# Strassen's algorithm for q, k and v, and attention in 64-wide tiles, in a transformer block in split fp32

## The chip, the cores and the metric

The kernel runs on one core of a Trainium2 chip. Its time is that of one execution on the device, in microseconds (us). TensorE multiplies matrices into PSUM, VectorE and ScalarE read PSUM and SBUF, GpSimd reads SBUF alone, and SyncE issues most of the DMAs.

## The reference

x has 32 sequences of 64 tokens and 1024 features. All in float32:

```
c  = x @ W1.T + b1 + 2 * (x @ A1[id]) @ B1[id]        # LoRA of rank 16, one adapter per sequence
q  = rope(c @ wq)  # 32 heads of 128;  k = rope(c @ wk), v = c @ wv: 8 heads, 4 q heads share one
o  = softmax(causal(q @ k.T / sqrt(128))) @ v         # within each sequence of 64
x1 = x + o @ wo
y  = x1 @ W2.T + 2 * gated LoRA (top 2 of 8 experts, rank 16, bias by language id)
out = x1 + y @ Wf.T + bf + 0.5 * gated residual (top 2 of 16 experts, rank 64)
```

## The kernel before, in words

Every large product is made of three matmuls: a float32 value is split into a high part, rounded to the fast format fp32r, and a low part, the remainder, and `three` (lines 527 to 531) adds hi x hi, hi x lo and lo x hi in PSUM. So a weight tile is loaded raw by SyncE, copied to its high part by ScalarE (`wd`, line 978, and `w_hi`, line 958) and subtracted to its low part by GpSimd (line 1193) or VectorE (`w_lo`, line 1294). There are two slots each for raw, hi and lo. A product bank is 128 outputs x 512 tokens; the four banks `PJ` are used in turn, and a bank is free when VectorE has taken it (the semaphore `taken`).

First, weights are folded once (W2 into Wf) and W1 and others are transposed through TensorE into DRAM scratch (`t_scratch`). Then come two halves of 1024 tokens each (an outer loop over `hf`), each in these stages:

1. The x blocks are loaded (`x_raw`, eight of 128 tokens), turned by TensorE, and split by ScalarE and VectorE; GpSimd adds them up again into x1, in SBUF.
2. The first projection, W1: eight weight tiles, each for two token halves, 24 matmuls and one fp32 LoRA matmul a bank (`w1_block`, line 662). VectorE splits these tiles.
3. Eight groups, one per kv head (loop at line 683): twelve banks of k, v and four q heads (24 matmuls each), with attention spread between them and into the group's output projection, 32 banks of 6 matmuls over the group's four heads, added to x1 by VectorE (line 1434). Attention works on blocks of 128 tokens, two sequences at once, the mask taking away what crosses: per unit of one head and 512 tokens, `score`, `turn_p` and `pv` are four fp32 operations of 128x128 each. VectorE rotates (`rotate`, line 1364), masks and takes maxima (`mask_and_max`), and normalises; ScalarE does the exponentials, copies transposed probabilities, and makes o's high part; VectorE makes its low part.
4. The second projection, its routing, and the output stage, which this change leaves nearly as they were.

Each engine works through its own list in order; only semaphores join them. `hold` puts an instruction of its own behind a wait.

## Time and profile before

| | us |
|---|---|
| median of 3 runs (2927.39 to 2931.74) | 2928.24 |
| span of the profiled execution | 2929.6 |
| TensorE busy in it | 2887.8 |
| VectorE busy | 1516.9 |
| ScalarE busy | 710.9 |
| GpSimd busy | 478.3 |

A matmul's recorded duration overlaps with the next one's, so starts are compared to find what one costs. An instruction's name gives the output and the inputs by the program's names, with the form; "PEld" is the load of a stationary operand. The granted clock is the share of full speed that TensorE was given.

### The profile page before, as it was taken

The page shows a single profiled execution, that of the slowest core. Times are in us where ns is not written, and L with a number is a line of the kernel's source. Part 1 is how long each engine was busy: PE and PEld are TensorE (multiplying, and loading weights), DVE is VectorE, ACT ScalarE, POOL GpSimd, SP SyncE. Part 2 cuts the span into 40 slices and gives each one's busy share as a digit, 9 for nine tenths or more (in the row PEclk, how much of TensorE's full clock was granted, in tenths as well). Part 3 has the DMA queues.
Part 4 walks back from the last instruction along what each step waited for, and adds up shares of the span by engine and source line. Part 5 has one row for each costly group of instructions (what it writes and reads, how often), then busy time and mean ns, then how long its engine had stood idle before and what let it go on. Part 6 is the DMA issues. An engine that isn't in the chain of part 4 may idle for free.

```text
span 2929.6 us, 39491 instructions
## 1 busy us (share of the span) xinstructions
PE 2887.8 (99%) x14200; PEld 2407.0 (82%) x14200; DVE 1516.9 (52%) x2443; ACT 710.9 (24%) x1681; POOL 478.3 (16%) x198
## 2 busy tenths in 40 slices
PE   8989999999999999999998999999999999999999
PEld 7867888888888888887876788888888888888887
DVE  2131656465665646565523265646556474656452
ACT  2121223132221313231102131313223131323110
POOL 0020111211111111110302012111111211111030
PEclk9999999999999999999999999999999999999999
DMA  6841111111111111111442111111111111110232
GB/s 214 233 121 37 43 44 36 43 43 42 37 43 43 36 43 43 37 35 55 111 144 60 43 37 49 37 43 36 43 43 36 44 39 45 37 43 29 72 99 68
DMA packets 230725, 174.67 MB, mean 60 GB/s; under 512 B 65146, under 2 KB 198394, under 8 KB 230658
## 3 DMA queue, kind: packets, MB, share of 16 engines
q1 hardware_dynamic: 202850, 151.80, 18.1%
q10 hardware_dynamic: 27808, 22.02, 2.3%
q8 instruction: 36, 0.59, 0.1%
q14 instruction: 31, 0.25, 0.0%
HBM read 151.58 MB, written 22.22 MB: 59 GB/s over the span
## 4 chain that ended last, share of the span: by engine, by line
PE 89%; DVE 5%; issue 2%; ACT 2%; SPq 1%; DMA 0%; ACTq 0%; DVEq 0%
PE prod L529 26%; PE prod L531 25%; PE prod L530 25%; PE turned L726 4%; PE turned L705 2%; PE turned L715 2%; ACT probs L1051 2%; DVE rope_sin L1372 2%; PE turned L523 1%; PE prod L625 1%; PE prod L888 1%; DVE row_max L1385 1%; DVE probs L1382 1%; PE turned L695 0%; PE prod L865 0%
## 5 line engine op out<-in xcount | busy, mean ns | idle before, releaser
L529 PE MATMUL prod<-c_hi,w_hi 128*128 128x512 f32 (+1 forms) x1856 | 737.7, 397 | 3.2 <-DVE c_lo L1445 3.2
L531 PE MATMUL prod<-c_hi,w_lo 128*128 128x512 f32 (+1 forms) x1856 | 724.3, 390 | 0.0
L530 PE MATMUL prod<-c_lo,w_hi 128*128 128x512 f32 (+1 forms) x1856 | 722.7, 389 | 0.0
L1193 POOL TENSOR_TENSOR w_lo<-raw,w_hi 128x1024 fp32r<-128x1024 f32 x160 | 382.1, 2388 | 1844.1 <-ACT w_hi L983 1844.1
L1434 DVE TENSOR_TENSOR x<-prod,x 128x512 f32<-128x512 f32 x512 | 349.4, 690 | 284.0 <-PE prod L531 281.4
L531 PEld LDWEIGHTS prod<-c_hi,w_lo 128*128 128x128 f32 (+1 forms) x1856 | 347.3, 187 | 75.9
L529 PEld LDWEIGHTS prod<-c_hi,w_hi 128*128 128x128 f32 (+1 forms) x1856 | 347.8, 187 | 74.1 <-DVE c_lo L1445 4.0
L530 PEld LDWEIGHTS prod<-c_lo,w_hi 128*128 128x128 f32 (+1 forms) x1856 | 348.1, 188 | 70.5 <-issue 1.0
L529 PE MATMUL prod<-o_hi,w_hi 128*128 128x512 f32 x1024 | 405.0, 395 | 0.0
L531 PE MATMUL prod<-o_hi,w_lo 128*128 128x512 f32 x1024 | 399.4, 390 | 0.0
L530 PE MATMUL prod<-o_lo,w_hi 128*128 128x512 f32 x1024 | 398.8, 389 | 0.0
L983 ACT CAST w_hi<-raw 128x1024 fp32r<-128x1024 f32 x160 | 167.5, 1047 | 509.1 <-PE prod L531 509.1
L529 PE MATMUL prod<-x_hi,w_hi 128*128 128x512 f32 x656 | 284.2, 433 | 5.4 <-DVE x_lo L1305 1.8
L1051 ACT ACTIVATE probs<-probs,neg_max 128x128 f32<-128x128 f32 x512 | 199.6, 391 | 356.9 <-DVE neg_max L1387 356.9
L531 PE MATMUL prod<-x_hi,w_lo 128*128 128x512 f32 x656 | 257.8, 393 | 0.0
L530 PE MATMUL prod<-x_lo,w_hi 128*128 128x512 f32 x656 | 257.2, 392 | 0.0
L1369 DVE TENSOR_TENSOR rope_cos<-prod,consts_sb 128x512 f32<-128x512 f32 x160 | 110.1, 688 | 246.7 <-PE prod L531 242.7
L531 PEld LDWEIGHTS prod<-o_hi,w_lo 128*128 128x128 f32 x1024 | 192.2, 188 | 41.1
L530 PEld LDWEIGHTS prod<-o_lo,w_hi 128*128 128x128 f32 x1024 | 192.6, 188 | 38.2
L529 PEld LDWEIGHTS prod<-o_hi,w_hi 128*128 128x128 f32 x1024 | 192.5, 188 | 37.9
L1372 DVE TENSOR_TENSOR rope_sin<-prod,consts_sb 64x512 f32<-64x512 f32 x320 | 220.2, 688 | 4.3
L529 PEld LDWEIGHTS prod<-x_hi,w_hi 128*128 128x128 f32 x656 | 124.2, 189 | 43.7 <-issue 18.8
(123 smaller groups left out, 2689.4 us busy)
## 6 DMA issues: line engine op xcount, KB each, us to landing
raw<-in_wq SPq DMA_DIRECT2D x64, 512.0 KB, 4.0
raw<-in_wo SPq DMA_DIRECT2D x64, 512.0 KB, 3.8
raw<-t_scratch SPq DMA_DIRECT2D x34, 512.0 KB, 3.5
t_scratch<-x ACTq DMA_DIRECT2D x17, 512.0 KB, 5.0
x_raw<-in_x SPq DMA_DIRECT2D x16, 512.0 KB, 8.8
raw<-in_wk SPq DMA_DIRECT2D x16, 512.0 KB, 3.6
raw<-in_wv SPq DMA_DIRECT2D x16, 512.0 KB, 3.6
raw<-m_scratch SPq DMA_DIRECT2D x16, 512.0 KB, 3.5
```

Source lines behind the costliest of these rows:

```text
L529: pe.matmul(dst, wh, xh, start=start, stop=False)
L530: pe.matmul(dst, wh, xl, start=False, stop=False)
L531: return pe.matmul(dst, wl, xh, start=False, stop=stop)
L705: mm = pe.matmul(SB_[u % 2][:, b * P:(b + 1) * P], Q[:, (u % 2) * NT + b * P:(u % 2) * NT + (b + 1) * P], K[:, t * NT + b * P:t * NT + (b ...
L715: mm = pe.transpose(TBK[:, b * P:(b + 1) * P], SM[:, c:c + P], ident)
L726: mm = pe.matmul(OB[:, b * P:(b + 1) * P], V[:, (t * BPT + b) * HD:(t * BPT + b + 1) * HD], PT[:, c:c + P], start=True, stop=True)
L983: act.copy(WH[j % 2][:], RAW[j % 2][:]).then_inc(wd_hi, 1)
L1051: ins = act.activation(SM[:, c:c + P], SM[:, c:c + P], ACT.Exp, bias=NMX[:, r:r + 1], scale=SM_SCALE, accum_out=SUM[:, r:r + 1])
L1193: pool.tensor_tensor(WL[j % 2][:], RAW[j % 2][:], WH[j % 2][:].bitcast(F32), ALU.subtract).then_inc(split_d, 1)
L1369: dve.tensor_tensor(view(RC[:, rs], SPT), src, cos, ALU.mult)
L1372: ins = dve.tensor_tensor(view(RS[a:a + hd2, rs], SPT), src[b:b + hd2], sin, ALU.mult)
L1434: dve.tensor_tensor(X1[:, xs], PJ[q % 4][:], X1[:, xs], ALU.add).then_inc(taken, 1)
```

## The change

- **q, k and v by Strassen's algorithm** (in Winograd's form, with shared sums). c is no longer one matrix but seven blocks of 512 features x 512 tokens: b11, b21, b22 and four sums t1 to t4, each split into hi and lo. They are made while W1 runs: W1's tiles are walked twice, first for the first 512 tokens, then for the second (`W1_ORDER`), so there are 16 tile loads a half; VectorE forms the sums. The weights come in pairs of 256 columns (k with v, or two q heads; `load_pair`), 24 pairs a half. GpSimd forms four sums and seven low parts for each pair, ScalarE seven high parts. TensorE makes seven products of 4 x 3 matmuls for a pair (`product`), where there were four banks of 24 matmuls. VectorE combines the seven products into four banks' worth with seven adds, and rotates out of PSUM.
- **Attention per sequence.** Scores are 64x64, two sequences in the two halves of the partitions and two heads side by side; `pv` contracts over the 64 keys of one sequence, for two heads at once. V is transposed a second time, shifted by 64 rows, so that every sequence's rows stand in either half. A group's attention is spread over its last pair and the next group's first two pairs (the last group's over the first output projection banks).
- **o goes through DRAM.** ScalarE copies and stores it in quarters (`o_out`). After the eight groups the output projection runs alone: four blocks of 1024 rows of wo, each of 16 banks x 24 matmuls; o is loaded back and split by ScalarE and GpSimd.
- **x1's start goes through DRAM.** GpSimd adds x's parts up, SyncE stores them (`store_xt`) and loads them before the output projection (`load_x1`).
- **W1's low parts** are made by GpSimd (`tile_lo`), in turn with those sums (`x_back`).
- The halves and groups are written out in full in place of loops, and the next half's first x blocks are turned inside the output stage.

The core of the diff (of the removed lines, the q, k, v loop alone):

```diff
-                    for j in range(12):
-                        main(Q_G + j, (j // TT) % 2, j % TT, CH, CL).then_inc(prod, 1)
...
+W1_ORDER = [(j, 0) for j in range(KC)] + [(j + 4 * s, 1) for j in range(KC // 2) for s in range(2)]
...
+BLOCKS = ["b11", "b21", "t2", "t3", "t1", "t4", "b22"]
+PR_1, PR_2, PR_6, PR_7, PR_5, PR_4, PR_3 = range(7)
...
+LOS = {0: 1, 1: 2, 2: 3, 4: 4, 3: 5, 5: 6, 6: 7}
...
+        places = ["b11", "t2", "b21", "t3", "t1", "t4", "b22"]
+        CBH = {b: sb(f"{b}_hi", [P, 4 * NT], F32R, offset=16 * i * KB) for i, b in enumerate(places)}
+        CBL = {b: sb(f"{b}_lo", [P, 4 * NT], F32R, offset=(16 * i + 8) * KB) for i, b in enumerate(places)}
...
+            def store_xt(hf, b):
+                sp.wait_ge(x_sum, hf * TB + b + 1)
+                sp.dma_start(xt_d.rearrange("k p n -> p k n")[:, :, b * P:(b + 1) * P], view(XS[b % 2][:], KC)
+                             ).then_inc(xt_out[b % 2], 16)
...
+            def load_pair(n, hf, g, qd):
+                if g == 0 and qd == 0:
+                    sp.wait_ge(w_lo, pool_no(hf, T_WO - 1) + 1)
+                else:
+                    sp.wait_ge(s_lo, 7 * (n - 1) + 6)
...
+            def load_o(hf, kb):
+                sp.wait_ge(o_stored, 16 * 4 * (hf * NKV + 2 * kb + 2))
+                if kb == 0:
+                    sp.wait_ge(qprod, q_done(pair_no(hf, NKV - 1, QD_23), 3))
+                elif kb == 1:
+                    sp.wait_ge(o_stored, 16 * 4 * (hf + 1) * NKV)
+                    sp.wait_ge(qprod, q_done(pair_no(hf, NKV - 1, QD_23), 6))
+                else:
+                    sp.wait_ge(prod, qbase(hf) + wo_q(kb - 2, KC - 1, TT - 1) + 1)
+                for c in range(KC):
+                    sp.dma_start(chunk_of(o_lows(kb % 2, OWP), c), o_d[kb * KC + c]).then_inc(o_in[c], 16)
...
+                for n in range(2, T_WO):
+                    if n - 2 < TB:
+                        store_xt(hf, n - 2)
+                    load_w1(hf, n)
...
+                def product(n, i, first):
+                    name, bank = BLOCKS[i], (7 * n + i) % 4
+                    gg, qd = divmod(n, QUADS)
+                    pg, pq = divmod(n - 1, QUADS)
+                    pe.wait_ge(s_lo, 7 * n + LOS[i])
...
+                    hold(pe)
+                    for k in range(4):
+                        if first:
+                            pe.wait_ge(cb_lo, hf * C_N + C_AT[name, k])
+                        ws, xs = slice(k * P, (k + 1) * P), slice(k * NT, (k + 1) * NT)
+                        mm = three(PJ[bank][:], SH[i][:, ws], SL[i][:, ws], CBH[name][:, xs], CBL[name][:, xs],
+                                   k == 0, k == 3)
+                    mm.then_inc(qprod, 1)
...
+                    for b in range(BPT):
+                        for r in range(2):
+                            for s in range(2):
+                                c = b * P + s * SEQ
+                                mm = pe.matmul(SCB[s * SEQ:(s + 1) * SEQ, b * P + r * SEQ:b * P + (r + 1) * SEQ],
+                                               Q[r][t][:, c:c + SEQ], K[:, t * NT + c:t * NT + c + SEQ],
+                                               start=True, stop=True)
+                    mm.then_inc(scores, 1)
...
+                    for b in range(2):
+                        for s in range(2):
+                            for r in range(2):
+                                rows = slice(r * SEQ, (r + 1) * SEQ)
+                                c = (2 * hb + b) * P + s * SEQ
+                                vv = v_block(2 * (t * BPT + 2 * hb + b) + s, r)
+                                o = b * P + s * SEQ
+                                mm = pe.matmul(view(OB[r], 2)[:, :, o:o + SEQ], VV[rows, vv:vv + HD],
+                                               view(PT[t][rows, :], 2)[:, :, c:c + SEQ], start=True, stop=True)
+                    mm.then_inc(pv_done, 1)
...
+                        for i in range(7):
+                            product(n, i, g == 0 and qd == 0)
+                            at_ = (qd, i)
+                            if g:
+                                if at_ == (QD_KV, 0):
+                                    turn_p(gg - 1, 0, 1)
+                                if at_ == (QD_KV, 1):
+                                    score(gg - 1, 1, 0)
+                                if at_ == (QD_KV, 3):
+                                    score(gg - 1, 1, 1)
+                                if at_ == (QD_KV, 5):
+                                    turn_p(gg - 1, 1, 0)
+                                if at_ == (QD_KV, 6):
+                                    pv(gg - 1, 0, 0)
+                                if at_ == (QD_01, 0):
+                                    pv(gg - 1, 0, 1)
+                                    turn_p(gg - 1, 1, 1)
+                                if at_ == (QD_01, 1):
+                                    pv(gg - 1, 1, 0)
+                                if at_ == (QD_01, 2):
+                                    pv(gg - 1, 1, 1)
+                            if at_ == (QD_01, 2):
+                                turn_v(gg, 0)
+                            if at_ == (QD_01, 3):
+                                turn_v(gg, 1)
+                            if at_ == (QD_01, 4):
+                                turn_v(gg, 2)
+                            if at_ == (QD_01, 5):
+                                turn_v(gg, 3)
+                            if at_ == (QD_23, 1):
+                                score(gg, 0, 0)
+                            if at_ == (QD_23, 3):
+                                score(gg, 0, 1)
+                            if at_ == (QD_23, 5):
+                                turn_p(gg, 0, 0)
...
+                for n in range(KC):
+                    c_hi(n)
+                    tile_hi(hf, n + 2, QN[f"c{n}.0"])
...
+                def o_out(gg, t, hb):
+                    w = 4 * gg + 2 * t + hb
+                    act.wait_ge(pv_done, w + 1)
+                    if w:
+                        act.wait_ge(o_stored, 16 * w)
+                    for r in range(2):
+                        ins = act.copy(OS_[:].rearrange("p (q r n) -> p r q n", q=2, r=2)[:, r], view(OB[r], 2))
+                    ins.then_inc(o_taken, 1)
+                    act.wait_ge(o_taken, w + 1)
+                    head = (gg % NKV) * GQ
+                    c = t * NT + hb * (NT // 2)
+                    act.dma_start(o_d.rearrange("h p n -> p h n")[:, head:head + GQ, c:c + NT // 2],
+                                  view(OS_[:], GQ)).then_inc(o_stored, 16)
...
+                x_back(0)
+                for n in range(2, T_WO):
+                    tile_lo(hf, n)
+                    if 1 <= n - 1 < TB:
+                        x_back(n - 1)
...
+                    pool.wait_ge(pair_in, 32 * (n + 1))
+                    pool.tensor_tensor(ta, a21, a22, ALU.add).then_inc(s_sum, 1)
+                    pool.wait_ge(s_sum, 4 * n + 1)
+                    pool.tensor_tensor(tb, ta, a11, ALU.subtract).then_inc(s_sum, 1)
+                    low(0, a11, 1)
+                    low(1, a12, 2)
+                    pool.wait_ge(s_sum, 4 * n + 2)
+                    low(2, tb, 3)
+                    pool.wait_ge(s_lo, 7 * n + 3)
+                    pool.tensor_tensor(tb, a12, tb, ALU.subtract).then_inc(s_sum, 1)
+                    low(4, ta, 4)
+                    pool.wait_ge(s_lo, 7 * n + 4)
+                    pool.tensor_tensor(ta, a11, a21, ALU.subtract).then_inc(s_sum, 1)
+                    pool.wait_ge(s_sum, 4 * n + 4)
+                    low(3, ta, 5)
+                    low(5, a22, 6)
+                    low(6, tb, 7)
...
+                    dve.wait_ge(rs_in, turn)
+                    dve.tensor_tensor(dst, dst, RS[:], ALU.add).then_inc(rotated, 1)
...
+                        def add(which, dst, i, other):
+                            dve.wait_ge(qprod, q_done(n, i))
+                            dve.tensor_tensor(dst, pj(i), other, ALU.add).then_inc(quad_in, 1)
...
+                        dve.wait_ge(p1_in, n + 1)
+                        add_head(A_C11, PR_2, X0[:], 0, 0, 0)
+                        add(A_U2, X0[:], PR_6, X0[:])
+                        if late:
+                            mask(4 * (gg - 1) + 2)
+                        if qd == QD_23:
+                            mask(4 * gg)
+                        dve.wait_ge(quad_in, quad_at(n, A_U2))
+                        add(A_U3, XU[:], PR_7, X0[:])
+                        dve.wait_ge(quad_in, quad_at(n, A_U3))
+                        add(A_U4, X0[:], PR_5, X0[:])
+                        if late:
+                            mask(4 * (gg - 1) + 3)
+                            normalise(4 * (gg - 1) + 2)
+                        if qd == QD_23:
+                            mask(4 * gg + 1)
+                            normalise(4 * gg)
+                        if kv:
+                            if gg:
+                                dve.wait_ge(v_turned, 4 * gg)
+                            add(A_C22, XB, PR_5, XU[:])
+                            add(A_C21, XC, PR_4, XU[:])
+                            dve.wait_ge(quad_in, quad_at(n, A_C22))
+                            dve.tensor_copy(VX[:, 0:SEQ], XB[:, NT - SEQ:NT]).then_inc(v_pad, 1)
+                        else:
+                            add_head(A_C22, PR_5, XU[:], 1, 1, 1)
+                            add_head(A_C21, PR_4, XU[:], 1, 0, 2)
+                        if late:
+                            normalise(4 * (gg - 1) + 3)
+                        if qd == QD_23:
+                            normalise(4 * gg + 1)
+                        dve.wait_ge(quad_in, quad_at(n, A_U4))
+                        add_head(A_C12, PR_3, X0[:], 0, 1, 1 if kv else 3)
```

## Rows read from the trace of the kernel before

**Rows 1.** The page, part 1: busy us (share), instructions
```profile
PE 2887.8 (99%) x14200; PEld 2407.0 (82%) x14200; DVE 1516.9 (52%) x2443; ACT 710.9 (24%) x1681; POOL 478.3 (16%) x198
```
**Rows 2.** The page, part 4: chain that ended last, share by engine
```profile
PE 89%; DVE 5%; issue 2%; ACT 2%; SPq 1%; DMA 0%; ACTq 0%; DVEq 0%
```
**Rows 3.** Timeline of TensorE: start us, duration us, engine line, output<-input
```profile
320.19 0.61 PE L705 MATMUL turned<-k_rot,q_rot 128*128 128x128 f32 x4
...
448.67 0.72 PE L705 MATMUL turned<-k_rot,q_rot 128*128 128x128 f32 x5
...
702.91 0.39 PE L529 MATMUL prod<-c_hi,w_hi 128*128 128x512 f32 x1
...
704.95 0.39 PE L529 MATMUL prod<-c_hi,w_hi 128*128 128x512 f32 x1
...
705.63 1.05 PE L705 MATMUL turned<-k_rot,q_rot 128*128 128x128 f32 x8
...
706.76 0.40 PE L530 MATMUL prod<-c_lo,w_hi 128*128 128x512 f32 x1
```
**Rows 4.** Windows: busy us (instructions) by engine, granted clock, DMA; one group
```profile
320.20:448.70 128.50, 128.25 (x650) 108.71 (x649) 75.30 (x122) 33.65 (x92) 23.89 (x10) 1.00 0.14 42
```
**Rows 5.** Groups of TensorE instructions: busy us, mean ns of one
```profile
L705 PE MATMUL turned<-k_rot,q_rot 128*128 128x128 f32 x1024 | 134.6, 274 | 0.0
L575 PE MATMUL prod<-small_t,raw 128*128 128x80 f32 x144 | 17.1, 272 | 0.0
```
**Rows 6.** Groups on VectorE
```profile
L1369 DVE TENSOR_TENSOR rope_cos<-prod,consts_sb 128x512 f32<-128x512 f32 x160 | 110.1, 688 | 246.7 <-PE prod L531 242.7
L1372 DVE TENSOR_TENSOR rope_sin<-prod,consts_sb 64x512 f32<-64x512 f32 x320 | 220.2, 688 | 4.3
L1382 DVE TENSOR_TENSOR probs<-turned,consts_sb 128x512 f32<-128x512 f32 x128 | 87.5, 683 | 0.0
L1385 DVE TENSOR_REDUCE row_max<-probs 128x4 f32<-128x512 f32 x128 | 87.9, 686 | 4.4
L1392 DVE RECIPROCAL row_rcp<-row_sum 128x4 f32<-128x4 f32 x128 | 22.6, 177 | 192.5 <-ACT probs L1051 192.5
L1394 DVE TENSOR_TENSOR probs<-probs,row_rcp 128x512 f32<-128x512 f32 x128 | 88.6, 692 | 4.4
```
**Rows 7.** Line 1376, least/median/greatest duration in ns
```profile
L1376 DVE TENSOR_TENSOR k_rot<-rope_cos,rope_sin x32: 691/1368/2052, 294.4 to 2585.5; 128x512 f32<-128x512 f32 x32
```
**Rows 8.** Groups on GpSimd
```profile
L1193 POOL TENSOR_TENSOR w_lo<-raw,w_hi 128x1024 fp32r<-128x1024 f32 x160 | 382.1, 2388 | 1844.1 <-ACT w_hi L983 1844.1
L1184 POOL TENSOR_TENSOR x<-x_hi,x_lo x16 | 43.0, 2688 | 287.8 <-DVE x_lo L1305 287.4
```
**Rows 9.** Groups on ScalarE
```profile
L983 ACT CAST w_hi<-raw 128x1024 fp32r<-128x1024 f32 x160 | 167.5, 1047 | 509.1 <-PE prod L531 509.1
L1044 ACT CAST o_hi<-turned 128x512 fp32r<-128x512 f32 x128 | 75.2, 587 | 112.1 <-PE turned L726 112.1
```
**Rows 10.** The page, part 6: DMA issues, KB each, us to landing
```profile
raw<-t_scratch SPq DMA_DIRECT2D x34, 512.0 KB, 3.5
t_scratch<-x ACTq DMA_DIRECT2D x17, 512.0 KB, 5.0
```
**Rows 11.** Timeline, TensorE and SyncE, two stretches
```profile
203.18 1.02 PE L625 MATMUL prod<-h_masked,lora_b 128*128 128x512 f32 x2
...
209.52 1.02 PE L625 MATMUL prod<-h_masked,lora_b 128*128 128x512 f32 x2
...
1549.92 16.71 SPq L438 DMA_DIRECT2D b_rows<-in_B  x16
```
**Rows 12.** The eight x blocks of a half, from issue to landing
```profile
DMA to landing us min/median/max: 3.4/8.8/14.2
```
**Rows 13.** Between the halves: TensorE in the timeline, then windows
```profile
1542.88 0.33 PE L523 MATMUL turned<-consts_sb,x_raw 128*128 128x128 f32 x1 [3.67 <-issue]
...
1539.00:1584.00 45.00, 36.01 (x167) 29.14 (x165) 18.38 (x15) 13.08 (x14) 21.96 (x8) 0.89 0.29 61
```

More of the change, by code:

```diff
@@ L206, in build @@
+        BC = [sb(f"c2_cols{i}", [P, P], offset=(196 + i) * KB) for i in range(2)]
+        RS = sb("rope_sin", [P, NT])
         CT = sb("consts_sb", [P, C_COLS])
@@ L1164, in _ @@
-                bases = b_bases(i)
-                for s in range(2):
-                    ffn_block(s, i * (2 * P) + s * P, *bases, last=(s == 1))
-                store(D - P, Q_O + 4 * KC - 2, q_base)
+                for s in range(KC):
+                    if s < KC - 1:
+                        tile_hi(hf, T_B + s + 1, Q_O - 1 if s == 0 else Q_O + 4 * (s - 1) + 1)
+                    if s:
+                        store(s - 1)
+                    if hf + 1 < HALVES and s >= 4:
+                        x_hi(hf + 1, s - 4)
```

1547 lines of the change are left out of this document (875 added, 672 removed).

## The prediction

> **What bounds the kernel now.** I read the page's busy shares first, then the chain of waits, the windows and timeline of one attention group, and last the rows for what is added. TensorE is busy 99% of the span [rows 1] and holds 89% of the chain [rows 2]. In the groups of q, k, v, attention and output projection, 16 of them, it never waits: a 128x512 matmul starts every 0.227 us (nine of them in 2.04 us), and one group takes 448.67 - 320.19 = 128.5 us, of which 480 x 0.227 = 109.0 us are the 512-wide matmuls and the rest, 19.5 us, attention's small ones [rows 3]. So each removed matmul is worth its 0.227 us, as long as the others keep up; VectorE is busy 75 of these 128 us, ScalarE 34, GpSimd 24 [rows 4]. The profiled execution has a span of 2929.6 us; the median of the runs is 2928.2, 1.4 less. The sum is made on the first.
>
> **1. Seven products for eight.** Per group q, k and v took 12 banks x 8 blocks x 3 = 288 matmuls; now three pairs x 7 products x 4 blocks x 3 = 252, the hi/lo triple kept. The output projection keeps its 1536 per half. 36 x 16 x 0.227 = -130.7 us.
>
> **2. Attention's own matmuls.** Per group before 32 scores, 32 P transposes, 32 PV, 8 V transposes. An fp32 matmul is two instructions, a transpose one. Eight instructions cost 706.76 - 0.227 - 705.63 = 0.90 us, 0.112 each [rows 3]. After: 64 scores of 64x64 (128 instructions), 32 PV (64), 16 + 16 transposes (32). PV and transposes still load or stream 128 columns: 96 x 0.112 = 10.8 us. No row shows 64 columns: below 0.056 (half), above 0.112; a moving side of 80 with 128 weight columns lasts 272 ns against 274 at 128 [rows 3, 5], so only a matmul narrow on both sides gets cheaper, which these are. I take 0.065: 8.3 us. Sum 19.1 against 19.5, -5 us in all; ends -24 and +90.
> The Trainium skill (TensorEngine Tiling (Array Packing), Key Properties) says that a change of tiling mode drains the engine, and that tiles work independently. No row of this case shows either; both are rivals below.
>
> **3. VectorE at the end of a group's last pair.** One head's sum is an add and a rotation, 0.69 + 0.69 + 2 x 0.69 + 0.69 = 3.5 us [rows 6]. Mask, maximum and its scaling take 0.68 + 0.69 + 0.18 = 1.6, normalising 0.18 + 0.69 = 0.9. In the last pair (heads 2 and 3) its order after the fifth product is: sum 0.7, mask(1) 1.6, normalise(0) 0.9, head 3.5, head 3.5, normalise(1) 0.9: 11.1 us. TensorE meanwhile has the sixth and seventh products (12 x 0.227 = 2.7 each), a transposition 0.45 and the next pair's first product, 8.6 us, and then transposes what normalise(1) makes. It also transposes normalise(0) after only 2.7 us, when VectorE needs 3.2. Four of VectorE's operations here read two SBUF operands, and those wait for GpSimd: the final add of a rotation took 0.69 alone and 1.37 or 2.05 beside a GpSimd operation [rows 7]. GpSimd now has 11 operations of about 1.3 us (half of 2.39 and its fixed part) in each pair of some 24 us [rows 8], busy 6/10, so 0.4 us each. VectorE 12.7, TensorE 9.4 with its own short wait: 3.3 us late, and 0.9 at each of the two other transpositions that follow a normalise closely. 5.1 x 14 junctions = +70 us; from 3.2 (no contention, 45 us) to 9 (every such operation waits out a whole GpSimd one, 126 us).
> The Trainium skill (SBUF — State Buffer, on the shared port pair) calls this an exclusive lock held for the whole instruction, by which the loser blocks. The trace agrees: 2.05 us is an operation of 0.69 behind a remainder of 1.36 [rows 7]. It speaks against this change, since 264 GpSimd operations per half now run in the group stage instead of 80.
>
> **4. Outputs through DRAM.** ScalarE copies four quarters of a group's output (about 0.8 us each) and stores each, 512 KB; it waits for the store before. Such a store took 5.0 us, under load [rows 9, 10]. TensorE asks for the next after 2.7 + 1.8 = 4.5 us. Three in a row lag by about 1 us in the end, seen by the V transposition behind them in ScalarE's queue: +14 us (14 groups), 0 to 35.
>
> **5. The first projection, W1.** Now each weight tile is loaded and split twice, 16 per half, by GpSimd (2.39) instead of VectorE. That alone fits under a product of 209.52 - 203.18 = 6.34 us [rows 8, 11]. But SyncE stores a block of x and then loads the next weight, in order; the store waits for GpSimd's sum of that block, which stands behind GpSimd's split of the tile before. For tiles 3 to 9 this closes a ring: sum 2.7, two issues 0.7, landing 3.5 (up to 5.5, as the 512 KB store goes ahead), hi copy 1.05, lo 2.39, hand-overs 0.3: 10.6 to 12.6, I take 11.0 [rows 8 to 10]. TensorE needs 7 x 6.34 + 5.4 (the second LoRA product) = 49.8 us where the ring takes 77: +27. To this +3.5 for tile 2, whose copy waits for the first product's end, and +4 for the second B1 rows, which SyncE issues only after tile 10 (8 of them 8.3 us, 16 took 16.7 [rows 11]). 34.5 per half, +69; 52 to 86. Queued behind SyncE's store wait are the W1 loads alone.
>
> **6. From W1 to the pairs.** The last two W1 banks now become four sums. In turn come six operations of about 0.7 us on VectorE (4.3), ScalarE's copy of the last sum (0.6), the first weight's hi (0.6), GpSimd's lo (1.3) and their hand-overs: the first product starts about 8 us after the last W1 bank. Before it followed at once. +8 per half, +16; 8 to 22.
>
> **7. Start of the output projection.** It now stands alone behind the groups and reads o back, eight loads of 512 KB. Eight such loads of x landed after 3.4 to 14.2 us [rows 12]. They are issued after the fourth of the last seven products; TensorE has 11 us left, then takes them block by block, so its first bank ends about 2 us late; the second waits for GpSimd, which first splits a weight (2.4) and then eight blocks at 1.3: 4 us. +6 per half, +12; 4 to 30. From then on a tile of 10.9 us hides its load and split.
>
> **8. Between the halves.** Before, TensorE idled 3.7 us and then went through x blocks one by one, slow clock included: the 45 us from the last output at 1539 held 30.6 of work (96 x 0.227 for two banks and two LoRA products, 1.7 for four fp32 matmuls, 8 x 0.89 for turning x), so 14 idle or slow [rows 13]. Now four x blocks are turned inside the output stage. The other four still wait for the copy of the LoRA rows (1.9, twice the 1.05 of half its size) and leave about 3: -11 us. In the first half x blocks 4 to 7 are loaded behind 16 LoRA loads (1 us each to issue, as the B1 rows [rows 11]): +3. Together -8; -16 to +5.
>
> **The sum.** -131 - 5 + 70 + 14 + 69 + 16 + 12 - 8 = +37 us: 2929.6 + 37 = 2966.6, on the scale of the median 2965. Only 131 us are removed, and the two rings on VectorE and SyncE give back 139.
>
> **Rivals.**
> A. Half-width tiles run two at a time (faster). Place: the scores and PV of all groups. If two of them overlap, 8.3 + 7.2 us a group become 7.8, -124 us: 2841. It decides from 2.3 us per group (37 us in all). For it: neighbours write different halves of the array; the same page of the Trainium skill has tiles load and multiply in parallel. Against: the 80-wide row shows that loading 128 weight columns, not streaming, sets the pace of PV [rows 5].
> B. VectorE is in time (faster). Place: step 3. If GpSimd is idle there and ScalarE's chain is short, steps 3 and 4 fall from 84 to 20 us: 2901. It becomes faster than before from 47 us of 84. Against: 11.1 over 8.6 stands without contention.
> C. Each entry into and exit from the half-width blocks drains the pipeline. A matmul lasts 0.39 but starts every 0.227 [rows 3]: a drain costs at least 0.16, at most 0.39; 16 per group: 41 to 100, take 60: 3025. Before, blocks of full-width small matmuls fit without such a loss. The page of the Trainium skill named in part 2 states such a drain, and by it this would come on top.
> D. The clock falls in the junctions. Before, after TensorE had idled 3.7 us, a stretch of 45 us had a mean granted clock of 0.89, that is a part of it at 1.2 instead of 2.4 GHz [rows 13]. If a wait of 3.3 us brings this on in 14 junctions, at 3.4 us lost each, +48: 3013. In W1's ring the same would be hidden, since 6.3 + 3.4 stays below 11.
> E. It doesn't do what it says: the pair loads (1 MB) and eleven GpSimd operations exceed a pair's time. Landing 7 us and 11 x 1.3 = 14.3 us make 21.3 against TensorE's 19.1 + 6.4 = 25.5: it fits, barely. GpSimd's operations 1.5 times as long would make 28.5, +3 us a pair, 48 pairs, +144: 3109.
>
> **How the numbers follow.** Forecast 0.44, A 0.10, B 0.20, C 0.13, D 0.08, E 0.05. Forecast's own range 2925 to 3010. Below 2885 lies most of A, above 3060 most of E and the long ends of C: range 2885 to 3060. A measurement tells 0.2% (6 us) from no change. Faster: A, most of B and 0.06 of the forecast, 0.34; same 0.04 between them; slower 0.62.
>
> **What would show it.** In the trace after: 4032 product matmuls for q, k, v in place of 4608; a W1 stage in which TensorE is busy about 6.3 of every 11 us for seven tiles, its waits on GpSimd's lo; a wait before the second P transposition of a group of 3 us on VectorE's normalise; a group (without output projection) of about 82 us against 84.9; score blocks of about 2.1 us for 32 instructions. The prediction is wrong if W1 shows no ring (then 2896), if the normalise wait is absent (B), or if small blocks cost far from 19 us a group (A, C).

## The result: 2.7% slower

The changed kernel took 3009.38 us in the median of 4 runs (3003.12 to 3012.09) against 2929.31 (2927.39 to 2931.74, 4 runs). The ratio is 1.0271, 95% interval [1.0256, 1.0286]: +80 us, where +36 had been forecast. The profiled execution has a span of 3010.0 us.

The page of the changed kernel answers to [rows 1, 2]: TensorE, then the shares of the chain that ended last.

```profile
PE 2733.9 (91%) x14520; PEld 2187.9 (73%) x14520; DVE 1352.2 (45%) x2011; ACT 871.5 (29%) x2089; POOL 1188.8 (39%) x790
PE 68%; DMA 7%; issue 7%; DVE 7%; POOL 6%; ACT 3%; SPq 1%; ACTq 0%; DVEq 0%; POOLq 0%
```

TensorE is busy 154 us less and the kernel is 80 us longer, so 234 us of idleness came in. TensorE went from 99% to 91%, and DMA, VectorE, GpSimd and bare issue hold a quarter of the chain. The windows say where. First three stretches of the kernel before: first half from about the first weight product on, its groups with output projection, and from the end of the first half's outputs to the second half's groups (the W1 stage, as the first row is). Columns: length, busy us (instructions) of TensorE, its weight loads, VectorE, ScalarE, GpSimd, then granted clock, DMA share, GB/s.

```profile
165.90:286.10 120.20, 118.60 (x495) 92.41 (x495) 29.14 (x30) 26.22 (x36) 18.74 (x7) 0.98 0.20 52
286.10:1316.20 1030.10, 1026.48 (x5187) 869.56 (x5185) 603.87 (x979) 278.48 (x754) 190.36 (x80) 1.00 0.14 40
1539.00:1672.50 133.50, 124.51 (x531) 97.37 (x529) 37.01 (x36) 31.13 (x41) 24.35 (x9) 0.96 0.20 52
```

The same stages in the changed kernel, with its products and its output projection apart. Its products start at 345.8 and 1762.6, the last one of the first half ends at 989, the output projection starts at 998.

```profile
165.90:345.80 179.90, 131.27 (x496) 99.24 (x494) 63.93 (x67) 39.61 (x51) 62.62 (x27) 0.86 0.32 91
...
345.80:989.00 643.20, 575.25 (x3667) 457.48 (x3668) 427.37 (x635) 256.61 (x786) 341.27 (x261) 0.99 0.21 69
...
998.00:1363.80 365.80, 361.12 (x1675) 295.57 (x1676) 60.10 (x89) 77.91 (x138) 151.04 (x92) 1.00 0.28 91
...
1591.00:1762.60 171.60, 132.39 (x496) 100.45 (x496) 63.98 (x70) 40.52 (x52) 68.59 (x28) 0.87 0.28 85
```

The W1 stage costs 345.8 - 286.1 = 59.7 us more in the first half and 171.6 - 133.5 = 38.1 in the second. Of the 59.7 us, 12.7 are busy time for about the same matmuls (131.27 against 118.60 us), at a granted clock of 0.86 in place of 0.98; the rest is idle. Products and projection take 1018 us (345.8 to 1363.8) against 1030: only 12 less, although 65 us of matmuls are gone from each half. The second half has the same shape: 1020.6 us (1762.6 to 2783.2).

**The W1 ring** is there as forecast, with a period of 11.65 us: SyncE's issues, tile after tile.

```profile
242.33 0.37 SPq L490 DMA_DIRECT2D xt_scratch<-x_sum  x1
242.75 0.58 SPq L460 DMA_DIRECT2D raw<-t_scratch  x1
253.95 0.37 SPq L490 DMA_DIRECT2D xt_scratch<-x_sum  x1
254.37 0.58 SPq L460 DMA_DIRECT2D raw<-t_scratch  x1
```

What TensorE waited for in this stage of the first half (us in total, times, longest):

```profile
PE prod L648 <- POOL w_lo L1416: 26.2, 7, 5.1
PE turned L642 <- DMA x_raw<-in_x: 10.6, 1, 10.6
PE prod L756 <- issue: 8.5, 1, 8.5
PE prod L648 <- POOL s_lo L1451: 7.8, 1, 7.8
```

In order: W1's low parts, of which the ring has five waits with 17.9 us, tile 2 has 3.8 and the very first tile 4.6; x block 4, loaded behind the sixteen LoRA A loads; the second B1 rows; the first pair's weights.

And what it waited for in most of the products (360 to 970 us):

```profile
PE turned L852 <- DVE probs L1696: 35.0, 21, 1.7
PE turned L870 <- issue: 12.0, 8, 1.5
PE turned L870 <- ACT v_tok L1227: 10.0, 7, 6.5
PE turned L887 <- ACT o_out L1235: 8.6, 8, 2.4
```

That is three waits a group for normalise (L852 is the P transposition), two for the V copies (L870) and one or two for the output copies (L887). In the whole execution normalise has 71.3 us (44 waits), the V copies 45.9, the output copies 16.9 and the scores 3.8.

**The small blocks** are far cheaper than taken. A score block and a PV block, each with its neighbours:

```profile
591.47 0.39 PE L650 MATMUL prod<-b_hi,s_lo 128*128 128x512 f32 x1
591.79 1.15 PE L837 MATMUL turned<-k_rot,q_rot 128*64 128x64 f32 x32
592.87 0.50 PE L648 MATMUL prod<-t_hi,s_hi 128*128 128x512 f32 x1
593.21 0.39 PE L649 MATMUL prod<-t_lo,s_hi 128*128 128x512 f32 x1
...
610.00 0.39 PE L650 MATMUL prod<-b_hi,s_lo 128*128 128x512 f32 x1
610.52 1.16 PE L887 MATMUL turned<-probs_t,v_tok 64*128 64x128 f32 x16
611.62 0.50 PE L648 MATMUL prod<-b_hi,s_hi 128*128 128x512 f32 x1
611.95 0.39 PE L649 MATMUL prod<-b_lo,s_hi 128*128 128x512 f32 x1
```

The score block costs 593.21 - 591.47 less two starts of 0.227, 1.29 us for 32 instructions; PV (16 instructions) 1.50 standing alone and 1.27 before a transposition, which then adds 0.43. Per group 4 x 1.29 + 4 x 1.4 + 8 x 0.43 = 14.2 us; the forecast had 19.1, the kernel before 19.5 [rows 3]. A group took 80.8 us (six groups between the pair loads issued at 450.15 and 935.14) where 82 had been forecast: small blocks 5 us cheaper, waits dearer.

**The account** of +80 us. Removed products -131. Small blocks (14.2 - 19.5) x 16 = -85. Waits in the products' stage: 643.2 - 168 x 12 x 0.227 - 104 (30 score, 28 PV, 61 transposition blocks) = 81.6 a half, +163; TensorE was idle for 643.2 - 575.25 = 68 of these 81.6 us, and the other 13.6 are busy time above the bare cost, partly stretches at half clock (346 to 350 and 380 to 390 us). Output projection: 9 us before it, 365.8 - 1536 x 0.227 - 9.5 (the last group's remaining small blocks) = 7.6 in it, +33. W1 stages +98. Together +78. The first half's figures are taken twice; the second half's stretches, 651.5 and 369.1 us against 652.2 and 365.8, allow that.

### The profile page after: what moved, and what is told of

It reads as the page before. It is cut to its first block, busy times and chain, and to the rows that moved or that the text cites. A ratio compares the mean times of both kernels' runs of the same rounds, so it can differ in the third digit from the quotient of the medians.

```text
span 3010.0 us, 37398 instructions
## 1 busy us (share of the span) xinstructions
PE 2733.9 (91%) x14520; PEld 2187.9 (73%) x14520; DVE 1352.2 (45%) x2011; ACT 871.5 (29%) x2089; POOL 1188.8 (39%) x790
## 4 chain that ended last, share of the span: by engine, by line
PE 68%; DMA 7%; issue 7%; DVE 7%; POOL 6%; ACT 3%; SPq 1%; ACTq 0%; DVEq 0%; POOLq 0%
PE prod L648 20%; PE prod L650 20%; PE prod L649 20%; DMA o_scratch<-o_out 6%; PE turned L837 2%; ACT o_out L1235 2%; POOL w_lo L1416 2%; POOL o_lo L1481 1%; DVE rope_sin L1663 1%; POOL x_sum L1434 1%; DVE neg_max L1689 1%; PE turned L642 1%; POOL s_lo L1451 1%; PE turned L870 1%; PE prod L1068 1%
## 5 line engine op out<-in xcount | busy, mean ns | idle before, releaser
L1451 POOL TENSOR_TENSOR s_lo<-w_sum,s_hi 128x512 fp32r<-128x512 f32 x192 | 250.9, 1307 | 303.9 <-ACT s_hi L1196 303.9
L1765 DVE TENSOR_TENSOR x<-prod,x 128x512 f32<-128x512 f32 x128 | 88.5, 692 | 594.6 <-PE prod L650 594.6
L648 PE MATMUL prod<-t_hi,s_hi 128*128 128x512 f32 x768 | 314.6, 410 | 0.0
L650 PE MATMUL prod<-t_hi,s_lo 128*128 128x512 f32 x768 | 302.4, 394 | 0.0
L649 PE MATMUL prod<-t_lo,s_hi 128*128 128x512 f32 x768 | 301.8, 393 | 0.0
L648 PE MATMUL prod<-b_hi,s_hi 128*128 128x512 f32 x576 | 234.9, 408 | 15.8 <-POOL s_lo L1451 15.8
L650 PE MATMUL prod<-b_hi,s_lo 128*128 128x512 f32 x576 | 226.1, 393 | 0.0
L649 PE MATMUL prod<-b_lo,s_hi 128*128 128x512 f32 x576 | 225.5, 391 | 0.0
L1451 POOL TENSOR_TENSOR s_lo<-raw_pair,s_hi 128x512 fp32r<-128x512 f32 x144 | 194.6, 1366 | 73.9 <-ACT s_hi L1196 73.9
L1210 ACT ACTIVATE probs<-probs,neg_max 128x64 f32<-128x64 f32 x512 | 170.9, 335 | 142.5 <-DVE neg_max L1689 142.5
```

The lines of the kernel that those rows point to most:

```text
L648: pe.matmul(dst, wh, xh, start=start, stop=False)
L649: pe.matmul(dst, wh, xl, start=False, stop=False)
L650: return pe.matmul(dst, wl, xh, start=False, stop=stop)
L1210: ins = act.activation(ss, ss, ACT.Exp, bias=NMX[:, r:r + 1], scale=SM_SCALE, accum_out=SUM[:, r:r + 1])
L1451: pool.tensor_tensor(view(SL[i][:], 4), src, view(SH[i][:].bitcast(F32), 4), ALU.subtract).then_inc(s_lo, 1)
L1765: dve.tensor_tensor(X1[:, xs], PJ[q % 4][:], X1[:, xs], ALU.add).then_inc(taken, 1)
```

## The experiments

All times stand beside 3009.4 us for the change, and ratios are to the kernel before.

**1. SyncE's order in the W1 stage.**

```
 for n in range(2, T_WO):
+    load_w1(hf, n)
     if n - 2 < TB:
         store_xt(hf, n - 2)
-    load_w1(hf, n)
```

> Edit: in the W1 stage SyncE issues the load of weight tile n before the store of x block n-2 (it was the other way round), nothing else. Theory (SyncE's order closes the ring): the load of a tile no longer stands behind GpSimd's sum of an x block, which stands behind the split of the tile before; the period of SyncE's loads falls from 11.65 us to below 7, TensorE's waits of 3 to 5.7 us before six products of each half (25 us a half) go, and with them the stretches at half clock behind them: 3009 - 50 (waits) - 10 to 20 (clock) = 2940 to 2950. Rival 1 (the ring is GpSimd and the landing, not SyncE's order): split 2.3 and sum 2.8 on GpSimd plus landing 4.7 still take 9 to 10 us a tile: 2990 to 3000. Rival 2 (clock alone): waits go but products stay at half clock: 2960.

Measured: 2951.18 us (ratio 1.0070 [1.0053, 1.0087]), -58. The waits on the low part, in the same stage:

```profile
PE prod L648 <- POOL w_lo L1416: 8.4, 2, 4.6
```

Two exchanged lines give back 58 of the 80 us. The profiled executions, 3010.0 and 2954.6 us long, divide it: TensorE's waits on the low part fell from 54.6 to 19.8 us over both halves and those for the B1 rows from 17.3 to 14.3, 38 together; its busy time fell from 2733.9 to 2719.8, 14, with the same 14520 instructions. The ring's waits are gone; the two left (4.6 and 3.8) are those for the first tile and for tile 2. The 14 us fit the clock: from 240 to 277 us, inside the ring, the mean granted clock was 0.78, so TensorE ran at 1.2 GHz for 2 x 0.22 x 37 = 16 of 37 us; here it was 1.00 from 215 to 261. Most of the rest are V and output copy waits, 3 us shorter.

**2. The other waits of that stage, by earlier loads.** Second B1 rows in a place of their own, issued at tile 7; x blocks 4 to 7 ahead of the LoRA A loads.

```
-    if n == 10:
-        sp.wait_ge(prod, q_base + QN["c7.0"] + 1)
+    if n == 7:
+        sp.wait_ge(a_lo, hf + 1)
...
         load_b1(hf, 1)
```

> Edit: e1_ring, and the second B1 rows have a buffer of their own and are loaded at tile 7 instead of after product c7.0, and in the first half x blocks 4 to 7 are loaded before the sixteen LoRA A loads. Theory: the waits of 8.9 and 9.1 us before the LoRA matmul of c0.1, and of 10.6 us for the x block at the start, go too: 8 of 8.9 twice, 8 of 10.6 once (LoRA A is needed 6 us later and may now be late by some us): 20 to 25 us below e1_ring. Rival (what is loaded earlier makes something else late: the A rows behind the x loads, the W1 tiles behind the B1 rows): within 8 us of e1_ring.

Measured: 2955.26 us (1.0088 [1.0070, 1.0106]): the rival. Both waits only changed their names. In the place of x_raw stands the LoRA product, and SyncE now spends 10.5 us on eight B1 issues just before it can issue the next weight tile, so that the waits on the low part rise from 8.4 to 16.2:

```profile
PE prod L654 <- POOL w_lo L1425: 16.2, 3, 7.8
PE prod L654 <- DVE lora_a_lo L1606: 10.5, 1, 10.5
...
239.51 10.50 SPq L488 DMA_DIRECT2D b_rows_t<-in_B  x8
250.05 0.58 SPq L461 DMA_DIRECT2D raw<-t_scratch  x1
```

**3. The same waits, by spreading the issues.**

```
-        load_b1(hf, 1)                       # eight in a row
+        load_b1(hf, 1, [n - 2])              # one after each weight load
...
-    tile_hi(hf, n + 2, QN[f"c{n}.0"])
+    tile_hi(hf, 2, QN["h0"])                 # ahead of the loop
...
+    if j == 3:
+        s_high(pair_no(hf, 0, 0), 0)         # ahead of the last W1 sums
```

> Edit: e1_ring with, in the W1 stage: the second B1 rows in a buffer of their own and issued one at a time between weight loads (in e2_w1 the eight together took SyncE 10.5 us and made tile 9 late by 8.4); weight tiles 2 and 3 issued before the first B1 rows; tile 2's hi copy released by the LoRA product instead of the first tile's own end; half of the first LoRA A loads issued by ScalarE; and the first pair's weight copied by ScalarE and split by GpSimd before the last W1 sums. Theory (these waits are all queue order): the waits of 11.1, 4.4, 7.5 and 8.4 us in the first half and 4.3, 7.5, 9.2 in the second fall to 5 us or so in all per half: -25 to -35 us under e1_ring, 2916 to 2926. Rival (the landings and the two-operand work of GpSimd and VectorE set the pace, each wait moves on as in e2_w1): 2945 to 2955.

Also in this version: weight tiles 2 and 3 are issued ahead of the first B1 rows, and ScalarE issues half of the first LoRA A loads.

Measured: 2926.45 us (0.9990 [0.9981, 1.0000]), 25 under experiment 1: the theory, at its upper end. In the first half the wait on the low part is 4.6 us, that before the pairs 5.7 in three pieces, that for the B1 rows gone. The start got worse, 17.3 us where it had been 12.1: turning x now waited for low parts (first row), and 2.1 for x itself, since ScalarE copies those x blocks behind the LoRA rows and their loads.

```profile
PE turned L651 <- DVE xt_lo L1614: 15.2, 2, 13.6
PE prod L657 <- POOL s_lo L1481: 5.7, 3, 2.4
PE prod L657 <- POOL w_lo L1446: 4.6, 1, 4.6
```

**4. VectorE's order.** normalise(v) ahead of sum U4 and mask(v+1); normalise(v+1) between the two heads.

```
+    normalise(4 * gg)
     add(A_U4, X0[:], PR_5, X0[:])
     mask(4 * gg + 1)
-    normalise(4 * gg)
     add_head(A_C22, PR_5, XU[:], 1, 1, 1)
+    normalise(4 * gg + 1)
     add_head(A_C21, PR_4, XU[:], 1, 0, 2)
-    normalise(4 * gg + 1)
```

> Edit: only VectorE's order in the pairs with attention: the first normalise of a pair is done before the sum U4 instead of after it and the second mask, the second between the two heads instead of after both. Theory (VectorE's order makes the P transposes late): TensorE's waits of 2 us before the P transposes on normalise (22 a half, 40 us a half by the excess over their minimum) fall below 0.4 each: -70 us, 2935 to 2945. Rival 1 (the softmax chain on ScalarE is as late: its exponentials end 3 us before the normalise): half of it, 2970. Rival 2 (what normalise no longer delays is made late instead: the heads, the banks they free, and the products behind them): 3000 to 3015.

Measured: 2982.90 us (1.0180 [1.0163, 1.0197]), -26.5, between the two rivals. Of the 35.0 us on normalise no row is left, and two waits stand in their place, PV on ScalarE's P copy and a score block (L837) held back by the previous mask:

```profile
PE turned L887 <- ACT probs_t L1219: 13.9, 7, 2.0
PE turned L870 <- issue: 11.9, 8, 1.5
PE turned L837 <- issue: 11.9, 7, 1.7
PE turned L870 <- ACT v_tok L1227: 10.8, 7, 6.1
PE turned L887 <- ACT o_out L1235: 6.0, 7, 1.7
```

**5. And these two taken away.**

```
+    p_out(4 * gg)                            # ahead of the exponentials
     exps(4 * gg + 1)
     s_high(n + 1, 5)
-    p_out(4 * gg)
...
-    if at_ == (QD_KV, 3):
+    if at_ == (QD_KV, 4):
         score(gg - 1, 1, 1)
```

> Edit: e3_norm, and what its trace shows to have come late in its place: ScalarE copies the first P transposition before the second set of exponentials instead of behind it, and the score block (KV, 3) comes one product later. In e3_norm these two cost 2.35 us (PV on ScalarE's copy) and 2.1 us (scores on the mask) a group. Theory (VectorE and ScalarE are each late only by their order, the work fits): both waits go, 4.4 us x 14 = -60 us under e3_norm, 2920 to 2930. Rival (VectorE is the limit there: it worked without a pause from 582.6 to 599.8 us of e3_norm's trace, so what is moved waits elsewhere): 2960 to 2975.

Measured: 2971.87 us (1.0147 [1.0130, 1.0164]), only 11 under experiment 4, nearer to the rival. P copy and scores fell to 2.0 and 0.3 us, and normalise stayed low (2.4), but the output copies rose from 6.0 to 15.1:

```profile
PE turned L887 <- ACT o_out L1235: 15.1, 15, 2.7
PE turned L870 <- issue: 12.0, 8, 1.5
PE turned L870 <- ACT v_tok L1227: 9.7, 7, 6.4
```

So the rival's time came out, but not by its mechanism: in these rows VectorE's part is gone and the next queue took over, ScalarE with its output copies. ScalarE's own waits for the stores hardly changed (30.1 and 31.9 us between 400 and 900 us).

**6. ScalarE's order.** V copy 0 ahead of the last output copy, V copy 2 ahead of a weight copy that waits for GpSimd.

```
+    v_out(gg, 0)
     o_out(gg - 1, 1, 1)
-    v_out(gg, 0)
...
     s_high(n + 1, 4)
+    v_out(gg, 2)
     s_high(n + 1, 3)
-    v_out(gg, 2)
```

> Edit: only ScalarE's order in the pair with the V transposes: the copy of V transposition 0 goes ahead of the copy of the last output quarter (which waits for a store), that of V transposition 2 ahead of a weight copy (which waits for GpSimd). Theory (V's copies are late for what stands before them in ScalarE's queue): TensorE's waits of 0.95 and 1.9 us before V transposes 1 and 3 go in 16 groups: -35 to -45 us, 2965 to 2975. Rival (TensorE's next wait takes it over: the output copy and the weight copies that now stand behind): below 10 us, about 3000 to 3009.

Measured: 2974.09 us (1.0145 [1.0128, 1.0162]), -35: the theory. TensorE's 22 us on V in this stretch fell to the 6.8 of one wait, with the others nearly as before (normalise 35.6, output copies 6.9).

**7. The output stores.** Each quarter copied and stored in two halves, a buffer and a semaphore each.

```
-    act.wait_ge(o_stored, 16 * w)
     for r in range(2):
-        ins = act.copy(OS_[:]..., view(OB[r], 2))
+        act.wait_ge(o_stored[r], 16 * w)
+        act.copy(OS_[r][:], OB[r]).then_inc(o_taken, 1)
```

> Edit: each output quarter is copied and stored in two halves with a buffer and a semaphore each, so that a half's store begins after its own copy. Theory (TensorE's waits on ScalarE's output copy, 1 us and 1.8 a group, come from the store, which took 5.2 us where it met the load of the next pair's weights and 3 us elsewhere): the next copy can begin 0.5 us earlier each time; -1 us a group, -10 to -16 us, 2993 to 2999. Rival (the store's landing beside the pair load is set by bytes, and two more issues of 0.37 us cost ScalarE what they gain): 3005 to 3015.

Measured: 2987.09 us (1.0201 [1.0185, 1.0216]), -22, more than expected: the waits on output copies fell from 8.6 to 3.0 us in this stretch, and six short V waits behind the copies went as well (of the 10.0 us on v_tok one wait of 6.3 is left).

**8. GpSimd's low parts.**

```
-    pool.tensor_tensor(view(SL[i][:], 4), src, view(SH[i][:]..., 4), ALU.subtract)
+    last = slice(0, P if n == pair_no(hf, 0, 0) else 1)
+    pool.tensor_tensor(view(SL[i][:], 4)[:, :, last], src[:, :, last], ..., ALU.subtract)
```

> Edit: in the pairs after each half's first, GpSimd subtracts one column in 128 instead of the whole block for the seven low parts of the weights (so the lows are left out; the sums stay). Theory (lock between VectorE and GpSimd: an addition of a rotation takes 0.69 us alone and 1.8 beside a GpSimd operation): VectorE's two-SBUF-operand work falls to 0.69, its chain in the last pair is 1.5 to 2 us shorter per group and the waits on normalise halve: -25 to -40 us, 2970 to 2985. Rival 1 (contention is off the path): 3000 to 3009. Rival 2 (GpSimd's lateness itself, for ScalarE's weight copies wait for its sums and V's copy waits behind them, is the larger part): -50 to -70, 2940 to 2960.

Measured: 2924.03 us (0.9981 [0.9972, 0.9991]), -85, more than any theory's. What TensorE still waited for in the products (360 to 970 us):

```profile
PE turned L852 <- DVE probs L1697: 21.5, 22, 1.7
...
PE turned L870 <- issue: 3.3, 8, 0.4
PE turned L870 <- ACT v_tok L1227: 2.0, 3, 1.2
PE turned L887 <- ACT o_out L1235: 1.4, 1, 1.4
```

In the whole execution normalise fell from 71.3 to 42.2 us, the V copies from 45.9 to 11.5, the output copies from 16.9 to 2.0, and TensorE's busy time by 11.0: 89 of the 89.8 us between the two spans.

VectorE's rotations hardly got shorter (the changed kernel, then this one, 400 to 940 us), but its scaling of the row maxima did:

```profile
L1666 DVE TENSOR_TENSOR q_rot<-q_rot,rope_sin 128x512 f32<-128x512 f32 x53 | 49.5, 935 | 1.8
...
L1689 DVE TENSOR_SCALAR neg_max<-row_max 128x8 f32<-128x8 f32 x28 | 26.9, 960 | 1.0
```

```profile
L1667 DVE TENSOR_TENSOR q_rot<-q_rot,rope_sin 128x512 f32<-128x512 f32 x56 | 50.0, 892 | 1.9
...
L1690 DVE TENSOR_SCALAR neg_max<-row_max 128x8 f32<-128x8 f32 x29 | 5.3, 182 | 1.0
```

So VectorE did wait for GpSimd, but at an operation that the prediction had priced at 0.18 us and the expectation did not name. In the changed kernel one such scaling, from 604.78 us on, took 1.26 us and ended within 0.02 us of the end of a GpSimd sum that had begun at 604.75; another, from 598.56 on, took 0.81 and ended with one as well. The exponentials wait for this scaling, and normalise waits for them. All 64 scalings together are 44 us shorter here (872 ns in the mean of the whole execution against 182), and no run takes this part away alone.

What changed besides is when the next pair's weights are loaded: SyncE waits for GpSimd's sixth low part. In the changed kernel the load is issued at 611.5 us, and ScalarE's first output store of that group follows at 612.8 into it; here the load goes out at 588.8 and the store at 591.2, 1.1 us later behind it. Landing of this first store, changed kernel and this one:

```profile
DMA to landing us min/median/max: 5.6/5.6/5.6
```

```profile
DMA to landing us min/median/max: 4.1/4.1/4.1
```

The first stores of the other groups of this half do the same, 5.5 to 5.7 us against 4.1 to 4.3 (the last group's 7.2 against 6.2); all later stores of a group but one (4.7) took 2.9 to 3.2 in both. So GpSimd's lateness reached TensorE by three ways: VectorE's scalings, a DMA collision with ScalarE's store wait behind it, and ScalarE's waits for GpSimd's sums. The rows give what TensorE waited for in the end, not how much each of these ways brought.

**9. The lock in the rotation.** The rotation's last addition reads one PSUM and one SBUF operand; where TensorE waited for `rs_in` it now waits for `rotated`.

```
+    ins.then_inc(sin_in, 1); dve.wait_ge(sin_in, turn)
+    dve.tensor_tensor(s3, s3, cos, ALU.mult).then_inc(rs_in, 1)
-    dve.tensor_tensor(dst, dst, RS[:], ALU.add).then_inc(rotated, 1)
+    dve.tensor_tensor(dst, src, RS[:], ALU.add).then_inc(rotated, 1)
```

> Edit: in VectorE's rotation the cosine product is written in place into the PSUM bank and the last addition reads bank + rope_sin, so that no operation of the rotation reads two SBUF operands; the bank is released by the addition, 0.7 us later. The same number of operations. Theory (the lock with GpSimd lengthens these additions: mean 0.94 us for q_rot, 1.8 beside a GpSimd operation, 10 a group): they fall to 0.69, 2 us a group on VectorE, half of it on the path: -15 us, 2990 to 3000, with the waits on normalise falling from 1.7 to about 1.2. Rival 1 (the lock is not on the path): 3005 to 3012. Rival 2 (banks freed 0.7 us later make products late): above 3015.

Measured: 3000.92 us (2998.52 to 3010.55; ratio 1.0244 [1.0228, 1.0259]), -8, an interval that touches that of the change: not decided here. The waits on normalise stayed (35.3 us in place of 35.0), and the scalings of the maxima, which this edit leaves alone, still took 916 ns in the mean. The additions did fall from 897 to 692 ns:

```profile
L1666 DVE TENSOR_TENSOR q_rot<-q_rot,rope_sin 128x512 f32<-128x512 f32 x128 | 114.8, 897 | 4.5
```

```profile
L1668 DVE TENSOR_TENSOR q_rot<-prod,rope_sin 128x512 f32<-128x512 f32 x128 | 88.6, 692 | 4.4
```

**10. Rival A by itself.**

```
-    for b in range(BPT):
-        for r in range(2):
-            for s in range(2):
+    for s in range(2):
+        for b in range(BPT):
+            for r in range(2):
```

> Edit: in a score block, only the order of its 16 score matmuls: the eight that write TensorE's lower 64 columns first, then the eight that write the upper ones (before, each neighbour wrote the other half). Same work, same data. Rival A of the prediction (half-width tiles run two at a time; in the trace neighbours start 6 to 7 ns apart and the pair 51 ns on): neighbours in one half can't overlap, the block of 1.15 us becomes 1.8 to 2.2: +0.65 to 1.05 us x 64 blocks = +40 to +65 us, 3050 to 3075. Other theory (narrow instructions are just cheap, 36 ns each): no change, 3003 to 3012.

Measured: 3060.88 us (1.0450 [1.0432, 1.0467]), +51.5. The block of 1.15 us now takes 1.90; 64 x 0.75 = 48.

```profile
602.01 1.90 PE L837 MATMUL turned<-k_rot,q_rot 128*64 128x64 f32 x32
```

That is 59 ns an instruction in place of 36. In a score block, neighbours that write different halves of the array do overlap. PV's order was not varied; its 1.16 us for 16 instructions against 0.112 each before only suggests the same.

**11. All of it together.** The edits of experiments 1 and 3 to 7, and at the output projection two more, which were not run alone:

```
-    sp.wait_ge(qprod, q_done(pair_no(hf, NKV - 1, QD_23), 3))
+    sp.wait_ge(qprod, q_done(pair_no(hf, NKV - 1, QD_23), 1))    # 3 only from chunk 4 on
...
-    pe.wait_ge(rs_in, rotated_at(last_gg, QD_23, 3))
+    pe.wait_ge(rs_in, rotated_at(last_gg, QD_23, 2 if q == Q_WO else 3))
```

> Edit: e7_w1, e6_norm, e4_vout (also V copy 0 ahead of the last output copy) and e11_split together, and at the start of the output projection: the reload of o's first four chunks begins after the product that frees their place (two products earlier), and the first bank waits for its own head instead of the last one. Theory (the waits are independent in place, so the gains add): 83 + 38 + 35 + 12 + 12 = 180 under 3009: 2830 to 2845, 3% below the kernel before. Rival (VectorE is the next bound: in e6_norm it worked without a pause for 17 of a group's 77 us, so fewer waits elsewhere expose it): 2860 to 2880.

Measured: 2820.88 us (0.9632 [0.9619, 0.9645]), -188.5, below the range expected. One by one the gains had been 83, 38, 35 and 22, 178 in all.

With the rotation of experiment 9 as well:

> Edit: c1_all with the rotation of e10_rope. Theory (with other waits gone VectorE's chain is closer to the path, so the lock counts more than in e10_rope): 10 to 20 us under c1_all. Rival (later release of banks counts more as well): equal to c1_all within 5 us or above.

Measured: 2804.60 us (0.9579 [0.9566, 0.9592]), 16 under the former, intervals apart. With the other waits gone the rotation's part of the lock counts; the scalings still take 651 ns. This version is 4.2% faster than the kernel before, with the same number of TensorE instructions as the change:

```profile
PE 2697.0 (96%) x14520; PEld 2175.2 (78%) x14520; DVE 1315.6 (47%) x2011; ACT 859.5 (31%) x2089; POOL 1177.4 (42%) x790
```

## Why the prediction came out too low

The sign was right and the reason (waits give back more than the removed matmuls) too. The sum of +37 was wrong in the size of its terms, in both directions: small blocks 80 us less than taken, waits in the products' stage (steps 3 and 4) 79 more, the output projection 21 more, the W1 stages 21 more. The two largest errors cancel; that the time still fell within the range stated is luck. The steps that failed are 2, which priced the small blocks without overlap, and 4, which put 14 us where the rows show 63.

- **Step 1**, products -131: right; 4032 of 4608 matmuls remain, at the same 0.227 us.
- **Step 2**, small blocks -5 (its own 0.4 a group would make -6): mis-sized, -85 measured. I held that a matmul narrow on one side only is not cheaper (the 80-wide row) and took 0.065 us for the others, without overlap. PV takes 1.4 us for 16 instructions, and experiment 10 shows overlap in the scores: **rival A's** mechanism with 0.10, which I had priced at -124. The page TensorEngine Tiling (Array Packing), Key Properties, of the Trainium skill has tiles run in parallel; experiment 10 bears this out for the scores. I gave more weight to a row of a full-height matmul than to that rule.
- **Rival C**, a drain: 0.32 + 0.34 - 2 x 0.227 = 0.2 us for entry and exit of a score block together, less than its least price of 0.16 each, and inside the 1.29.
- **Step 3**, +70: right in size, 71.3 us of waits on normalise, though as 3 x 1.7 us a group and not as 3.3 and twice 0.9. But experiment 4 shows that taking them away was worth only 26 us, for two other waits took their place.
- **Step 4**, +14: this step failed most among the waits. TensorE waited 45.9 us for V copies and 16.9 for output copies, 63 in all. Step 4 saw just the stores' own queue. It missed that V copies 0 and 2 stand in ScalarE's order behind a store wait and behind a copy that waits for GpSimd (35 us by experiment 6), and that pair load and output store collide. With 3.8 us at the scores these are 138 of the 163 us; the other 25 or so are mostly busy time above the bare cost.
- The reason given in step 3, VectorE's additions waiting for GpSimd at 0.4 us each: they fall from 0.90 us to 0.69 without a second SBUF operand, 0.2 each. The price of that in this kernel was about 8 us, not resolved alone, and 16 once the path was short. The exclusive lock that the Trainium skill states (SBUF — State Buffer, Terms) agrees with this. The larger part was elsewhere: step 3 counted the scaling of the maxima at 0.18 us, and beside GpSimd it took 0.87. Without GpSimd's low parts it took 0.18 again, and the waits on normalise fell by 29 us (experiment 8), though other things changed with it.
- **Step 5**, W1 ring 69: the ring is right (11.65 us against 11.0). The waits of the first half were 17.9 us for the ring (27 forecast), 3.8 for tile 2 (3.5) and 8.5 for the B1 rows (4), 30.2 in all against 34.5. The ring's waits are shorter because part of each period went into matmuls at 1.2 GHz, which the forecast had run at full speed.
- **Steps 6 and 8**, +16 and -8: W1 to pairs 7.8 a half, right. At the start of the first half x waited 10.6 instead of 3, and the first tile's low part, which the forecast did not count, 4.6. With the drop to half clock, which I had called hidden in the ring, this is where steps 5, 6 and 8, +77, became +98: **rival D's** mechanism in another place. D's price of 3.4 us a junction had no row beside it. At the junctions it did not happen, with waits of up to 1.8 us:

```profile
395.00:935.00 540.00, 484.14 (x3194) 384.45 (x3196) 376.52 (x558) 226.61 (x711) 290.83 (x222) 1.00 0.20 63
```

- **Step 7**, +12: +33; 9 us before the first bank in each half, of which 8.6 on VectorE's last head, which the forecast did not count, and 7.6 later.
- **Rival B**, VectorE in time: refuted, the waits were there. **Rival E**: GpSimd's work did fit into a pair's time, but experiment 8 shows that being on time on average was not enough.

## What to carry to other kernels

Price a removed matmul by what its neighbours' queues then do: here -216 us of TensorE work became +80, and queue order, earlier loads, a split store and one PSUM operand, with the same matmuls, turned that into -124. The waits on normalise, removed alone, were worth 26 us where their rows said 71, since two waits of 2.0 and 1.7 us a group took the place of three; after each removal list the waits again, and add gains only where their places are apart. Ask of every queue what stands behind an instruction that waits on another engine: two exchanged lines on SyncE were worth 58 us. And when an engine gets more work, compare the mean duration of every kind of instruction on its neighbours, the short ones too: here one of 0.18 us had grown to 0.87.

## What the runs showed of the hardware

- Matmuls with 64x64 outputs in different halves of the array overlapped: 32 instructions in 1.15 us, against 1.90 when neighbours wrote the same half.
- VectorE's scaling of 128x8 maxima (one input, in SBUF) took 182 ns in the mean where GpSimd had little to do and 872 in the changed kernel, ending with the GpSimd operation beside it in the two cases looked at. Additions with two inputs in SBUF took 897 ns, with one of them in PSUM 692.
- A 512 KB store mostly took 2.9 us with no load in flight, 5.5 to 5.7 when issued 1.3 us behind a 1 MB load, and 4.1 to 4.3 when 2.4 us behind it.
- In the ring, waits of 2.3 to 3.7 us at intervals of about 11.6 us went with a mean granted clock of 0.78 (240 to 277 us). Three waits of 1.7 us and some shorter ones in each 81 us of the products' stage left it at 1.00 (395 to 935 us).
